# Routed experts of a decoder: 71 tiles of 256 rows in place of 39 of 512

## What is computed

```python
def _ffn(x, w1, w2, w3):
    return jax.nn.silu(x @ w1.T) * (x @ w3.T) @ w2.T      # w1, w3: 256 x 128, w2: 128 x 256
logits = xf @ router_w.T + expert_bias
rw, sel = jax.lax.top_k(logits, 2)
rw = jax.nn.softmax(rw, axis=-1)
combine = einsum('tk,tke->te', rw, one_hot(sel, 8))
for e in range(8):
    acc = acc + combine[:, e][:, None] * _ffn(xf, w1[e], w2[e], w3[e])
out = acc + shared(xf)
```

## Time and profile before

| what | us |
|---|---|
| time, median of 3 runs | 2847.98 (2846.27 to 2854.24) |
| span of the profiled execution, first to last instruction | 2842.9 |
| `route_and_share`, last scatter issued at | 793.9 |
| `run_experts`, first load issued to last scatter issued | 805.0 to 1040.2 |
| first load of `phase_scan` issued at | 1053.5 |

### The profile page before, as it was taken

The page is one execution under the profiler, slowest core; times in us unless marked ns, Lnnn a source line. Parts: engine busy times, 40 slices in busy tenths (PEclk is TensorE's granted clock), DMA queues, the critical chain, the costliest instruction groups (busy, mean ns, idle before and its releaser), DMA issues. The chain is left out here.

```text
span 2842.9 us, 43587 instructions
## 1 busy us (share of the span) xinstructions
PE 2473.1 (87%) x13058; PEld 1470.2 (52%) x13058; DVE 2260.3 (80%) x3693; ACT 1704.9 (60%) x3383; POOL 2044.5 (72%) x1817
## 2 busy tenths in 40 slices
PE   7969999989979966898989989899989999995665
PEld 5646666656646642333433333333358878873222
DVE  5879999756634449999999999999857777776887
ACT  7847787744312326667676676776555565654665
POOL 5529999757746655999999999999636666664554
PEclk9969999989989988999999999999999999997555
DMA  5911111001145535555455454555523332320000
GB/s 166 422 57 23 24 23 24 8 29 42 43 114 161 160 102 186 184 184 189 178 181 187 176 194 169 196 187 189 185 79 89 90 85 86 88 81 27 19 18 23
DMA packets 238423, 331.81 MB, mean 117 GB/s; under 512 B 46433, under 2 KB 186998, under 8 KB 217346
## 3 DMA queue, kind: packets, MB, share of 16 engines
q1 hardware_dynamic: 227538, 311.48, 33.1%
q0 software_dynamic: 9088, 16.94, 1.7%
q10 hardware_dynamic: 1584, 0.79, 0.1%
HBM read 231.45 MB, written 99.50 MB: 116 GB/s over the span
## 5 line engine op out<-in xcount | busy, mean ns | idle before, releaser
L1875 POOL TENSOR_TENSOR s_drive<-s_du,s_b_sb 128x1024 f32<-128x1024 f32 x256 | 600.6, 2360 | 40.2 <-DVE s_state_ps L2242 40.1
L2242 DVE TENSOR_TENSOR_SCAN s_state_ps<-s_decay_ps,s_drive 128x512 f32<-128x512 f32 x416 | 487.1, 1216 | 43.4 <-ACT s_decay_ps L2028 34.5
L2390 PE MATMUL s_y_ps<-s_read,w_ident 128*128 128x512 f32 x832 | 405.6, 613 | 90.6 <-DVE s_read L2255 90.4
L2028 ACT ACTIVATE s_decay_ps<-s_delta,neg_rate 128x508 f32<-128x508 f32 x512 | 340.6, 682 | 151.3 <-DVE s_state_ps L2242 93.4
L2390 PEld LDWEIGHTS s_y_ps<-s_read,w_ident 128*128 128x128 f32 x832 | 149.0, 191 | 323.0 <-DVE s_read L2255 186.5
L2255 DVE TENSOR_TENSOR s_read<-s_state_ps,s_c_sb 128x1024 f32<-128x1024 f32 x208 | 254.5, 1224 | 7.2
L1421 POOL DMA_INDIRECT m_y_scratch<-e_y,e_index x156 | 152.8, 979 | 93.5 <-DVE e_y L1467 51.7
L2679 POOL TENSOR_TENSOR c_share<-c_p,c_norm 128x1232 f32<-128x1232 f32 x64 | 148.6, 2322 | 83.2 <-DVE c_norm L2811 83.2
L742 ACT ACTIVATE b_pT<-b_turn_ps 77x512 f32<-77x512 f32 x256 | 144.5, 592 | 74.2 <-PE b_turn_ps L871 74.2
L2879 PE MATMUL c_f_ps<-c_ctxT,w_c_wqk 128*128 128x308 f32 x512 | 179.0, 438 | 8.1 <-DMA c_ctxT<-in_ctxT_dram 5.2
L1045 POOL DMA_INDIRECT m_rows_scratch<-m_xs,m_index x128 | 128.4, 1003 | 60.4 <-issue 39.8
(11 more groups left out here) (389 smaller groups left out, 6203.4 us busy)
## 6 DMA issues: line engine op xcount, KB each, us to landing
s_b_sb<-s_bc_scratch SPq DMA_DIRECT2D x64, 1024.0 KB, 6.3
s_c_sb<-s_bc_scratch SPq DMA_DIRECT2D x64, 1024.0 KB, 5.4
c_vp_scratch<-s_stage SPq DMA_DIRECT2D x152, 256.0 KB, 2.3
c_vp<-c_vp_scratch SPq DMA_DIRECT2D x64, 576.0 KB, 4.1
m_rows_scratch<-fill SPq DMA_DIRECT2D x33, 1040.0 KB, 26.8
e_w<-in_m_we_dram SPq DMA_DIRECT2D x39, 384.0 KB, 3.2
e_xg<-m_rows_scratch SPq DMA_DIRECT2D x39, 260.0 KB, 3.4
s_read<-m_y_scratch SPq DMA_DIRECT2D x32, 256.0 KB, 3.1
```

The costliest lines, as they stand in the source:

```text
L1875: nc.gpsimd.tensor_tensor(drive[:, (g * states + n) % drives, :, :], du[:, s, :, :], b_sb[:, n, :].unsqueeze(1).broadcast_to([128, halves, ...
L2028: nc.scalar.activation(decay[:, m, :, 1:], delta[:, s, m, :].rearrange("p (b t) -> p b t", t=T)[:, :, 1:], ACT.Exp, scale=core.neg_rate[:, ...
L2242: nc.vector.tensor_tensor_scan(home[:, h, :], decay[:, h, :, :].rearrange("p b t -> p (b t)"), drive[:, (g * states + n) % drives, h, :], ...
L2390: last = nc.tensor.matmul(y_ps[:, m, :], core.ident[:, :], read[:, r % deep, m, :], start=False, stop=False)
```

## The change

The routed experts run in tiles of `ET` = 256 rows, 64 + 7 = 71 of them. Each tile's rows are 130 KB, its weights are the same 384 KB. The two halves of the gate lie side by side in one PSUM bank, likewise the two of the value; both have two banks, used in turns. So SiLU and the product are each one instruction of 512 columns per tile, the matmuls of gate and value have 256 columns, there are two transposes, four matmuls back and two scatters per tile. Rows and results have 8 slots, weights 4. Transposes run two tiles ahead, and PE's order in iteration t is `up(t)`, `turn_x(t + 2)`, `down(t - 1)`. SP's order is as it was, and the wait ahead of the weights of tile t is now for `downed` of tile t - 4.

```diff
+ET = 256
+LONGEST = B * T // ET
+TILES = 2 * B * T // ET + 7
...
 def run_experts(core, table, y_dram):
-    halves = 2
-    x_slots, w_slots, y_slots = 5, 3, 5
+    halves, lots = 2, ET // 128
+    x_slots, w_slots, y_slots = 8, 4, 8
...
-        g_ps = ps("e_g_ps", [128, halves, GT])
-        u_ps = ps("e_u_ps", [128, halves, GT])
-        o_ps = ps("e_o_ps", [128, 2, GT])
-        turn_ps = ps("e_turn_ps", [128, GT])
+        g_ps = ps("e_g_ps", [128, 2, halves * ET])
+        u_ps = ps("e_u_ps", [128, 2, halves * ET])
+        o_ps = ps("e_o_ps", [128, 2, 512])
+        turn_ps = ps("e_turn_ps", [128, 2, 512])
...
                 sp.dma_start(xg[:, t % x_slots, :, :],
-                             core.rows_dram[ds(first, GT), :].rearrange("(b p) d -> p b d", b=GB)
+                             core.rows_dram[ds(first, ET), :].rearrange("(b p) d -> p b d", b=lots)
                              ).then_inc(x_in[t % x_slots].sem, 16)
                 if t >= w_slots:
                     sp.wait_ge(downed.sem, downed.at(t - w_slots, 1))
...
-                for j in range(GB):
+                for j in range(lots):
                     nc.gpsimd.indirect_dma_start(
...
+            def open_gate(t):
+                act.wait_ge(g_ready.sem, g_ready.at(t, 1))
+                if t >= 2:
+                    act.wait_ge(h_ready.sem, h_ready.at(t - 2, 1))
+                nc.scalar.activation(silu[:, t % 2, :], g_ps[:, t % 2, :], ACT.Silu).then_inc(silu_ready.sem, 1)
...
             for t in range(TILES):
                 take_index(t)
-                hidden(t, 0)
+                hidden(t)
                 if t >= 1:
                     weigh(t - 1)
-                hidden(t, 1)
...
+            def up(t):
                 pe.wait_ge(xT_ready.sem, xT_ready.at(t, 1))
                 landed(pe, w_in, t)
+                if t >= 2:
+                    pe.wait_ge(h_ready.sem, h_ready.at(t - 2, 1))
+                for n in range(halves):
+                    gate = nc.tensor.matmul(g_ps[:, t % 2, n * ET:(n + 1) * ET], w[:, t % w_slots, n, :],
+                                            xT[:, t % 2, :], start=True, stop=True)
+                gate.then_inc(g_ready.sem, 1)
+                for n in range(halves):
+                    value = nc.tensor.matmul(u_ps[:, t % 2, n * ET:(n + 1) * ET], w[:, t % w_slots, halves + n, :],
+                                             xT[:, t % 2, :], start=True, stop=True)
+                value.then_inc(u_ready.sem, 1)
...
             turn_x(0)
+            turn_x(1)
             for t in range(TILES):
-                if t + 1 < TILES:
-                    turn_x(t + 1)
-                up(t, 0)
+                up(t)
+                if t + 2 < TILES:
+                    turn_x(t + 2)
                 if t >= 1:
                     down(t - 1)
-                up(t, 1)
             down(TILES - 1)
```

More of the change, by code:

```diff
@@ L22 @@
 REGION = B * T
-LONGEST = B * T // GT
-TILES = 2 * B * T // GT + 7
+ET = 256
+LONGEST = B * T // ET
+TILES = 2 * B * T // ET + 7
 FILL_ROWS = 16
@@ L1238, in make_table @@
                 nc.vector.tensor_tensor(start[:, :], t_of, start[:, :], ALU.subtract)
-                nc.vector.tensor_scalar(owner[:, :], owner[:, :], float(REGION // GT), None,
+                nc.vector.tensor_scalar(owner[:, :], owner[:, :], float(REGION // ET), None,
                                         ALU.mult).then_inc(table_steps.sem, 1)
@@ L1243, in make_table @@
                 step(9)
-                nc.vector.tensor_scalar(table[0][:, :], start[:, :], float(routed * REGION // GT), float(GT),
+                nc.vector.tensor_scalar(table[0][:, :], start[:, :], float(routed * REGION // ET), float(ET),
                                         ALU.min, ALU.mult)
@@ L1357, in from_zero @@
             return landings[-1]
-        xg = sb("e_xg", [128, x_slots, GB, ROW])
+        xg = sb("e_xg", [128, x_slots, lots, ROW])
         w = sb("e_w", [128, w_slots, 3 * halves, 128])
[L1361 to L1365, removed]
-        g_ps = ps("e_g_ps", [128, halves, GT])
-        u_ps = ps("e_u_ps", [128, halves, GT])
-        o_ps = ps("e_o_ps", [128, 2, GT])
-        turn_ps = ps("e_turn_ps", [128, GT])
+        xT = sb("e_xT", [128, 2, ET])
+        silu = sb("e_silu", [128, 2, halves * ET])
+        h = sb("e_h", [128, 2, halves, ET])
+        y = sb("e_y", [128, y_slots, lots, D])
+        index = sb("e_index", [128, y_slots, lots], U32)
+        g_ps = ps("e_g_ps", [128, 2, halves * ET])
+        u_ps = ps("e_u_ps", [128, 2, halves * ET])
+        o_ps = ps("e_o_ps", [128, 2, 512])
+        turn_ps = ps("e_turn_ps", [128, 2, 512])
         x_in = [sig(f"e_x_in{n}", 16) for n in range(x_slots)]
@@ L1375, in run_experts @@
         xT_ready = sig("e_xT_ready")
-        up_ready = sig("e_up_ready", halves)
-        silu_ready = sig("e_silu_ready", halves)
-        h_ready = sig("e_h_ready", halves)
+        g_ready = sig("e_g_ready")
+        u_ready = sig("e_u_ready")
+        silu_ready = sig("e_silu_ready")
+        h_ready = sig("e_h_ready")
         downed = sig("e_downed")
@@ L1381, in run_experts @@
         y_ready = sig("e_y_ready")
-        scattered = [from_zero(f"e_scattered{n}", 16 * GB) for n in range(y_slots)]
+        scattered = [from_zero(f"e_scattered{n}", 16 * lots) for n in range(y_slots)]
         def landed(eng, slots, t):
@@ L1388, in all_scattered @@
         def all_scattered(eng, t):
-            eng.wait_ge(scattered[t % y_slots].sem, scattered[t % y_slots].at(t // y_slots, 16 * GB))
+            eng.wait_ge(scattered[t % y_slots].sem, scattered[t % y_slots].at(t // y_slots, 16 * lots))
         open_signals(nc, signals, [])
@@ L1432, in copy_xT @@
                 if t >= 2:
[L1433 to L1440, removed]
+                    act.wait_ge(u_ready.sem, u_ready.at(t - 2, 1))
+                nc.scalar.activation(xT[:, t % 2, :], turn_ps[:, t % 2, 0:ET], ACT.Copy).then_inc(xT_ready.sem, 1)
+            def open_gate(t):
[3 more added lines that the diff above has]
+                nc.scalar.activation(silu[:, t % 2, :], g_ps[:, t % 2, :], ACT.Silu).then_inc(silu_ready.sem, 1)
             copy_xT(0)
+            copy_xT(1)
             for t in range(TILES):
-                if t + 1 < TILES:
-                    copy_xT(t + 1)
-                for n in range(halves):
-                    open_gate(t, n)
+                open_gate(t)
+                if t + 2 < TILES:
+                    copy_xT(t + 2)
         @block.vector
@@ L1455, in take_index, with hidden @@
                 nc.vector.tensor_copy(index[:, t % y_slots, :], xg[:, t % x_slots, :, D]).then_inc(indexed.sem, 1)
-            def hidden(t, n):
-                dve.wait_ge(silu_ready.sem, silu_ready.at(t, n + 1))
+            def hidden(t):
+                dve.wait_ge(silu_ready.sem, silu_ready.at(t, 1))
+                dve.wait_ge(u_ready.sem, u_ready.at(t, 1))
                 if t >= 2:
                     dve.wait_ge(downed.sem, downed.at(t - 2, 1))
-                nc.vector.tensor_tensor(h[:, t % 2, n, :], silu[:, n, :], u_ps[:, n, :],
-                                        ALU.mult).then_inc(h_ready.sem, 1)
+                nc.vector.tensor_tensor(h[:, t % 2, :, :].rearrange("p n c -> p (n c)"), silu[:, t % 2, :],
+                                        u_ps[:, t % 2, :], ALU.mult).then_inc(h_ready.sem, 1)
             def weigh(t):
                 dve.wait_ge(downed.sem, downed.at(t, 1))
-                for j in range(GB):
+                for j in range(lots):
                     last = nc.vector.tensor_scalar(y[:, t % y_slots, j, :], o_ps[:, t % 2, j * D:(j + 1) * D],
@@ L1482, in turn_x @@
                 landed(pe, x_in, t)
[L1483 to L1486, removed]
+                if t >= 2:
+                    pe.wait_ge(xT_ready.sem, xT_ready.at(t - 2, 1))
+                for j in range(lots):
+                    last = nc.tensor.transpose(turn_ps[:, t % 2, j * 128:(j + 1) * 128], xg[:, t % x_slots, j, 0:D],
                                                core.ident[:, :])
                 last.then_inc(x_turned.sem, 1)
-            def up(t, n):
+            def up(t):
                 pe.wait_ge(xT_ready.sem, xT_ready.at(t, 1))
                 landed(pe, w_in, t)
[L1493 to L1497, removed]
+                if t >= 2:
+                    pe.wait_ge(h_ready.sem, h_ready.at(t - 2, 1))
[7 more added lines that the diff above has]
+                value.then_inc(u_ready.sem, 1)
             def down(t):
-                pe.wait_ge(h_ready.sem, h_ready.at(t, halves))
+                pe.wait_ge(h_ready.sem, h_ready.at(t, 1))
                 if t >= 2:
                     pe.wait_ge(y_ready.sem, y_ready.at(t - 2, 1))
-                for j in range(GB):
+                for j in range(lots):
                     for n in range(halves):
@@ L3512, in layout @@
         "m_tile_of": c(np.tile(np.arange(TILES, dtype=np.float32), (128, 1))),
```

(2 more changed lines are left out.)

## The result

| what | before | after |
|---|---|---|
| median us (lowest to highest, runs) | 2848.66 (2843.97 to 2854.24, 20) | 2856.36 (2850.74 to 2862.68, 20) |
| span of the profiled execution | 2842.9 | 2858.9 |
| first load of the experts to first load of the scan | 805.02 to 1053.50 | 805.02 to 1062.57 |

The ratio is 1.0025 with an interval of 1.0019 to 1.0031: the changed kernel is 7.7 us slower (5 to 9), just inside what was called no change (8.5 us), and 7 us above the forecast of 2849. The profiled execution of after took 2860.68 us, 4.3 over its median, and the stages with unchanged code don't last equally long in the two profiles. So I compare the expert stage alone: its two ends say **+9.1 us**.

A forecast was written before the change was run, and what follows sets the result against it. The prediction took PE to bound the expert stage, without a hole; -23 us without waits, +21.7 for waiting on rows and +2 for scatter gave +1 us, forecast 2849 us, range 2832 to 2866 for 8 in 10.

The forecast's parts named there:

- PE's work: Expert stage: 71 tiles of 2.84 us instead of 39 of 5.66, 19.1 us less.
- The sum without waits: All terms of the expert stage together if PE never waits: -23 us.
- The new wait: PE's transposes wait for rows issued too late by SP; period = max(2.84, (3.31 + landing) / 2), 21.7 us back.
- Landing of 130 KB: A tile's row load in the expert stage takes 3.0 us to land, against 3.5 for 260 KB.
- Landings scatter: Row loads' landings vary and PE feels late ones more than early ones: 2 us more.
- End of the stage: Expert stage's last wait for `e_h`, last scaling and the transposes done ahead: together 1.3 us less.
- POOL's last scatters: After the last `e_y`, POOL has two scatters at 1.28 us instead of four: 2.6 us less.
- Start: First `up` of the expert stage: smaller loads and two transposes fewer make some 0.8 us less.
- Semaphores: The stage has 5 more to raise and 8 more to clear: 0.8 us more, from a span of 0 to 1.7.
- A median landing of 2.5 or less: Faster rival: rows land in time for PE; at 2.5 us -16.5 us, 2831; below 2.37, 2825; chance 27%.
- a landing that doesn't depend on the size: Slower rival: rows still land in 3.5 us, PE stands in nearly every second tile; +18 us, 2866; chance 25%.
- The clock: Rival: holes in PE's work lower its clock in the expert stage, costing some hundred us; chance 3%.

The follow-up runs named there:

- rows_ahead: The changed kernel with SP loading the rows of tile t + 1 ahead of the wait for the weights' slot of tile t; 2825.89 us, ratio 0.9917 to before.
- five_weight_slots: The changed kernel with 5 weight slots instead of 4, nothing else; 2825.47 us, ratio 0.9925 to before.
- registers_ahead: The changed kernel with tile t + 1's two registers read ahead of the weights' slot wait, order of loads kept; 2831.05 us, ratio 0.9941 to before.
- turn_late: The changed kernel with PE's transposes turn_x(t + 2) moved behind the way back down(t - 1); 2837.82 us, ratio 0.9958 to before.
- small_weights: The changed kernel loading only 64 KB instead of 384 KB of each expert's weights from tile 4 on; 2833.38 us, ratio 0.9948 to before.
- three_weight_slots: The changed kernel with 3 weight slots instead of 4; 3060.63 us, ratio 1.0736 to before.

## Why the prediction was right or wrong

*PE's work, -19.1 us: right.* A tile without wait takes 2.84, the 256-column record 0.215 (taken: 0.218 as a middle, and 2.84 for the tile). *The sum without waits, -23 us: right.* rows_ahead and five_weight_slots are the case without waits, and stand 21.6 and 22.1 below the kernel before.

*The new wait: right in place and cause.* Transposes wait for the rows, at L1488 and nowhere else; SP's gap is as it was; the slot wait is the lever, in both directions (three slots +213 us against before, five -22), and so are each of the other terms of the formula: the reads of the registers (registers_ahead), the place of the transposes (turn_late), the landing (small_weights).

*Landing of 130 KB, 3.0: right.* The median is 2.9, and the mean of the stage's 45 row loads whose landing the trace shows is 3.06. The quiet slope that I took it from gave 0.5 for 130 KB less, and the median fell by 0.6. That the two are so near is in part luck: the DMA share rose from 0.57 to 0.69 at the same time, and no run changes the size alone, with the traffic as it was. The estimate from the Trainium skill's figures ("DMA: Bandwidth & Descriptors", Anatomy of one DMA) was 3.2 and about +8 us. Its time is the one that came, its landing is not. With the measured mean the excess is that of the forecast, and the missing 7 us came from the next step.

*Landings scatter, 2 us more: wrong; this is the failed step.* I had read 2.9 to 4.6 before, and treated the scatter as a small correction to a mean. But the period has a floor: a row that lands early wins nothing below 2.84, one that lands late costs all of its lateness. With the 45 measured landings put one after the other into the prediction's recurrence (next way back = the later of the last one + 2.84, and issue + landing + 1.2, where 1.2 is 0.05 to start and the measured 1.16, against the prediction's 1.26), 69 periods exceed 2.84 by 32.0 us in all; with their mean for each, by 21.6. The trace has 30.5. For the 26 other loads it shows no landing, but 19 of them ended a wait of the weight loads and can be read from its end: 2.6 to 5.1, 3.2 in the mean. With these in their places the recurrence gives 30.4, and their mean 22 to 23, by what is taken for the last seven. So the spread costs some 7 to 10 us, not 2, and that is most or all of the 6.8 by which the waits exceeded the forecast. Two runs show it without this reckoning: in turn_late and in registers_ahead landings of up to 3.6 cost nothing, and the medians are 3.3 and 3.2; with a slowest of 4.9 the excess is 11 us, with one of 3.9 it is 2.5. The tail had also grown: before, a tenth of the loads took over 3.72 us, in after over 4.16, although each is half as large. In the packets' records of the two traces, 845 to 1010 us, the 3072-byte packets of the weights that took over 0.7 us number 170 in after and 64 before, 2.7% and 1.7% of them; that these hold up the rows behind them fits with small_weights, where the tail shrank to 4.0, but it was not tested apart.

*End of the stage.* First `up` to last `e_y` is +10.0, and -19.1 - 1.3 + 30.5 is +10.1, so the 1.3 us of the last wait and scaling stand.

*POOL's last scatters, -2.6 foretold, -1.1 found.* With 2.57 us of POOL in 2.62 to 2.84 it had the least room, and the last tiles came one right behind the other; when the last `e_y` was done, POOL was still at the one before, so three scatters stood behind it and not two. *Start, -0.8 foretold, +0.1 found*: the second rows landed 3.4 us after their issue and not in less than 2.8.

*Semaphores, +0.8 foretold, 0 found in the sum, by luck:* the stretch from the last scatter to the scan is 12.4 us both times, but in the traces' records of the sequencers POOL clears 29 semaphores in 2.03 us instead of 21 in 1.33, and SP raises the next stage's 73 in 4.68 instead of 4.23. These 1.15 us are hidden by POOL's drain ahead of the clearing, which took 3.47 instead of 4.62. It takes 4.62 in both kernels with 512-row tiles and 3.47 or 3.48 in all those with 256-row tiles; why is open.

Together: +6.8 for the waits, +1.5, +0.9 and -0.8 make the +8.4 between the sum of the forecast (+0.7 before rounding) and the +9.1 of the trace. The sign "stage to about 1036" did not follow from the sum, which puts the last `e_y` near 1038 and the last scatter near 1040; they came at 1045.6 and 1049.2.

*The table* cost nothing: the last of its instructions is at 788.89, and DVE's next work waits for PE until 790.55.

*The rivals.* A median landing of 2.5 or less came in no run with after's traffic; but the -23 us that it rested on are real. Against a landing that doesn't depend on the size stands the median, 2.9. The clock didn't fall in after: 1.00 with holes of up to 2.1 us in 40 of 69 periods. The Trainium skill's page on TensorE ("TensorE: Matmul & The Clock Gate", A second HAM failure mode) describes a kernel that cycles through PSUM banks and whose clock oscillates under frequent short idles between groups. The trace of after, with frequent short idles that are waits for a DMA, keeps 1.00. The clock of three_weight_slots does swing, with 2.3 us of wait in every tile, but that too is a wait for a DMA and so not the page's case; no run here shows that one.

## What to carry to other kernels

Where one engine issues several streams of loads in one list, ask of each load which wait of another stream it stands behind; a load that is "prefetched" by eight slots can still leave one slot wait too late. Halving the tile halves the time that covers a landing, but not the landing: reckon the slack in us before and after, and if it comes near zero, issue earlier (another order, one slot more) in the same change; here that turned +8 into -22 us. And where a period has a floor, take landings by their distribution and not by their mean.

## What was not expected of the hardware

- The landing of the same 130 KB follows the traffic around it: median 2.4 us at a DMA share of 0.40 (small_weights), 2.5 at 0.36 (three_weight_slots), 2.9 at 0.69 (after), 3.3 at 0.77 (turn_late), 3.2 at 0.78 (registers_ahead), 3.4 at 0.78 (five_weight_slots), 3.2 at 0.81 (rows_ahead). Among the dense ones the share does not order them. The spread of 1.0 is more than halving the load gained (3.5 to 2.9), and turn_late paid some of its gain back in this way; rows_ahead and five_weight_slots had room for it.
- PE's granted clock held at 1.00 through frequent short holes, and swung, 0.67 in one stretch of 10 us and 1.00 in the next, when every tile of 6.3 us had a wait of 2.3 us (the windows of three_weight_slots above). In the first PE is busy for 8.03 of 10 us, in the second for 5.46, with about as many records: the same work takes longer and the wait is shorter in turn. Against the 5.75 us of the reckoning the clock cost some 0.5 us per tile.
